# Summing four expert answers per token: four VectorE additions against one fetch and three adding transfers

## The reference, cut to what matters

```python
gath = y[sorted_e, jnp.minimum(pos, CAP - 1)]              # every answer of an expert
out = jnp.zeros((T, Hq), x.dtype).at[tok].add(gath * wv[:, None])   # four answers per token are summed
sh = jax.nn.sigmoid(x @ w_shared_gate) * (jax.nn.silu(x @ sw_gate) * (x @ sw_up) @ sw_down)
x = x + jnp.tanh(g_ffn[0]) * (... out + sh ...)
x = x + jnp.tanh(g_xattn[1]) * _L1_xattn_ref(..., _layernorm(x, axis=-1), ctx_2048)
```

## Time and profile before

| what | us |
|---|---|
| median of three runs (lowest, highest) | 1172.74 (1171.52, 1173.14) |
| the profiled execution, first to last instruction (its span) | 1171.5 |
| TensorE busy (share of the span) | 1066.6 (91%) |
| VectorE busy | 956.1 (82%) |
| ScalarE busy | 892.2 (76%) |
| GpSimd busy | 702.5 (60%) |

### The profile page before, as it was taken

The page is one execution under the profiler, slowest core; times in us unless marked ns, Lnnn a source line. Parts: engine busy times, 40 slices in busy tenths (PEclk is TensorE's granted clock), DMA queues, the critical chain, the costliest instruction groups (busy, mean ns, idle before and its releaser), DMA issues.

```text
span 1171.5 us, 24138 instructions
## 1 busy us (share of the span) xinstructions
PE 1066.6 (91%) x8396; PEld 608.8 (52%) x8396; DVE 956.1 (82%) x1748; ACT 892.2 (76%) x1546; POOL 702.5 (60%) x626
## 2 busy tenths in 40 slices
PE   8988898889988988898889988999999999999995
PEld 5743444444444444444444447756654455557774
DVE  6999999999999999999999996853328888843335
ACT  4779999999999999999999996635534567734440
POOL 3016888888787878787878785457641001543331
PEclk9999999999999999999999999799999999999998
DMA  6797987888788888888776664867937003433326
GB/s 192 121 163 146 171 171 162 171 171 173 161 171 171 173 164 173 173 169 164 155 118 110 112 109 65 244 182 213 316 98 300 1 0 85 138 102 101 102 89 222
DMA packets 388928, 176.36 MB, mean 151 GB/s; under 512 B 330542, under 2 KB 373779, under 8 KB 388809
## 3 DMA queue, kind: packets, MB, share of 16 engines
q1 hardware_dynamic: 382104, 157.85, 62.2%
q0 software_dynamic: 6480, 16.77, 4.2%
q10 hardware_dynamic: 224, 0.20, 0.1%
HBM read 52.70 MB, written 43.59 MB: 82 GB/s over the span
## 4 chain that ended last, share of the span: by engine, by line
PE 51%; DVE 33%; ACT 5%; issue 5%; DMA 3%; POOL 2%; SPq 1%; POOLq 0%; ACTq 0%; DVEq 0%
DVE top L426 26%; PE bank L234 10%; PE bank L220 9%; PE bank L1187 4%; PE bank L2599 4%; PE bank L252 4%; PE bank L1580 3%; PE bank L2615 3%; PE bank L1174 2%; PE bank L1166 2%; ACT weight L485 2%; PE bank L270 1%; PE bank L1598 1%; PE bank L682 1%; POOL dispatched_rows L1823 1%
## 5 line engine op out<-in xcount | busy, mean ns | idle before, releaser
L485 ACT ACTIVATE weight<-bank,bias,sq_all 128x1024 uint8<-128x1024 f32 x512 | 610.2, 1201 | 24.1 <-PE bank L234 18.9
L426 DVE TENSOR_REDUCE top<-bank 128x1 f32<-128x512 f32 (+1 forms) x683 | 610.1, 951 | 11.9 <-PE bank L220 1.6
L537 POOL CAST weight<-turned 128x2048 bf16<-128x2048 uint8 x256 | 479.4, 1895 | 44.8 <-PE bank L252 23.2
L234 PE MATMUL bank<-kT,query 128*128 128x512 bf16 x1024 | 307.7, 382 | 11.8 <-ACT weight L485 4.8
L252 PEld LDWEIGHTS bank<-v_sb,weight 128*128 128x128 bf16 x4096 | 172.0, 97 | 103.4 <-POOL weight L537 1.9
L220 PE MATMUL bank<-kT,qspace 64*128 64x512 bf16 x687 | 134.9, 386 | 55.0 <-DVE top L426 55.0
L252 PE MATMUL bank<-v_sb,weight 128*128 128x16 bf16 x4096 | 172.5, 170 | 0.6 <-POOL weight L537 0.6
L220 PE MATMUL bank<-kT,query 128*128 128x512 bf16 x337 | 127.8, 379 | 1.6 <-DVE top L426 1.4
L234 PEld LDWEIGHTS bank<-kT,query 128*128 128x128 bf16 x1024 | 59.8, 96 | 103.8 <-ACT weight L485 61.8
L1823 POOL DMA_INDIRECT dispatched_rows<-qspace,put x32 | 37.1, 1161 | 117.8 <-DVE qspace L2376 108.6
L485 ACT ACTIVATION_READ_ACCUMULATOR weight<-bank,bias,sq_all 128x1 f32 x512 | 101.3, 198 | 0.0
(11 more groups left out here) (350 smaller groups left out, 1466.2 us busy)
## 6 DMA issues: line engine op xcount, KB each, us to landing
dispatched_rows<-zeros SPq DMA_DIRECT2D x32, 524.0 KB, 3.2
answered_rows<-zeros SPq DMA_DIRECT2D x16, 512.0 KB, 3.2
late<-answered_rows SPq DMA_DIRECT2D x16, 512.0 KB, 6.3
erow<-dispatched_rows SPq DMA_DIRECT2D x39, 131.0 KB, 2.1
wgu<-in_L_ffn_w_gate SPq DMA_DIRECT2D x26, 176.0 KB, 3.9
wgu<-in_L_ffn_w_up SPq DMA_DIRECT2D x26, 176.0 KB, 3.9
query<-qspace SPq DMA_DIRECT2D x32, 128.0 KB, 3.1
turned<-weight SPq DMA_TRANSPOSE x256, 3.1
```

Of the source, the lines that this page charges most:

```text
L234: mm = pe.matmul(unit[u % 2][:, v * 512:(v + 1) * 512], query2[:, t % 2, h, :], kT[:, h // 2, first + v * 512:first + (v + 1) * 512], star ...
L426: ve.tensor_reduce(top[:, first:first + count], bank[:, first % 3:first % 3 + count, :], AX.X, ALU.max).then_inc(s_max, 1)
L485: ac.activation(weight8[:, n % BYTES, u * 1024:(u + 1) * 1024], unit[u], ACT.Exp, bias=bias[:, n:n + 1], scale=sq_all[:, n:n + 1], accum_o ...
L537: po.tensor_copy(weight[:, n % 3, :, :, :].rearrange("p c q two -> p (c q two)"), turned8[:, n % 3, :, :].rearrange("p c q -> p (c q)").bi ...
```

## The change

The reading order of the table `answered` changes. For each group of four tiles, SyncE fetches the first choice's answers alone (one DMA, 512 KB, rows of 1 KB) into `answer_sums`, which lies in `late[:, 0:4, :]` and holds all 16 tiles. POOL then issues, for choices 1, 2 and 3 and for the four groups in turn, a DMA with `accum_op=ALU.add` that adds the answers of that choice to the same place. Each waits for the transfer before it on the same group. VectorE makes one addition of 128x1024 numbers for each group in place of four. ScalarE's `fade` and POOL's own work wait for the last adding transfer of group 0 in place of group 0's fetches. The waits at the end of the program (`finish_half`) change their counts only, as `s_got` is now raised once for each group here.

```diff
+                    def choices_added(k):
+                        return 16 * (E0 // FLYING + k - 1)
+
+                    answer_sums = late[:, 0:4, :].rearrange("p a (b c) -> p (a b) c", c=C)
+
+                    def tiles_of(g):
+                        return slice(g * G, (g + 1) * G)
+
+                    def choice_answers(g, k):
+                        return answered[g * G * P * K0:(g + 1) * G * P * K0, :].rearrange("(t p k) c -> p t k c", p=P, k=K0)[:, :, k, :]
...
-                        def fetch_answers(t):
-                            if t >= 2 * G and t % G == 0:
-                                sp.wait_ge(sm_["groups_combined"], t // G - 1)
-                            sp.dma_start(late[:, t % 8, :], answered[t * P * K0:(t + 1) * P * K0, :].rearrange("(p k) c -> p (k c)", k=K0)).then_inc(s_got[t // G], 16)
-
-                        for t in range(2 * G):
-                            fetch_answers(t)
+                        for g in range(NG):
+                            sp.dma_start(answer_sums[:, tiles_of(g), :], choice_answers(g, 0)).then_inc(s_got[g], 16)
...
-                        for t in range(2 * G, NT):
-                            fetch_answers(t)
...
-                        po.wait_ge(s_got[0], 16 * G)
+                        for k in range(1, K0):
+                            for g in range(NG):
+                                if k == 1:
+                                    po.wait_ge(s_got[g], 16)
+                                else:
+                                    po.wait_ge(s_er[g], choices_added(k))
+                                po.dma_start(answer_sums[:, tiles_of(g), :], choice_answers(g, k), accum_op=ALU.add).then_inc(s_er[g], 16)
+                        po.wait_ge(s_er[0], choices_added(K0))
...
-                        ac.wait_ge(s_got[0], 16 * G)
+                        ac.wait_ge(s_er[0], choices_added(K0))
...
-                            ve.wait_ge(s_got[g], 16 * G)
-                            for k in range(K0):
-                                settle()
-                                m = ve.tensor_tensor(x_sb[:, g * G:(g + 1) * G, :], x_sb[:, g * G:(g + 1) * G, :],
-                                                     late[:, (g % 2) * G:(g % 2 + 1) * G, k * C:(k + 1) * C], ALU.add)
-                                if k < K0 - 1:
-                                    step(m)
-                            m.then_inc(sm_["groups_combined"], 1)
+                            ve.wait_ge(s_er[g], choices_added(K0))
+                            ve.tensor_tensor(x_sb[:, tiles_of(g), :], x_sb[:, tiles_of(g), :], answer_sums[:, tiles_of(g), :],
+                                             ALU.add).then_inc(sm_["groups_combined"], 1)
```

More of the change, by code:

```diff
@@ L1138, in weights_loaded @@
                 return 64 * n + (16 if s < 2 * NG + 3 else 0)
-            s_er = [sem(f"x0_rows_fetched_{s}") for s in range(FLYING)]
+            s_er = [sem(f"x0_rows_fetched_then_answers_added_{s}") for s in range(FLYING)]
             s_er1 = s_ew[0:RING1]
@@ L2728, in experts1_vector @@
                             ve.wait_ge(sm_["shared_answers_added"], 2 * NG * G - (1 if g == 0 else 0))
-                            ve.wait_ge(s_got[g], 32 * G)
+                            ve.wait_ge(s_got[g], 16 * (G + 1))
                             finish_half(2 * g)
```

## The result

| | us |
|---|---|
| before, median (lowest, highest) of 4 | 1172.13 (1170.89, 1173.14) |
| after, median (lowest, highest) of 4 | 1205.43 (1201.75, 1206.47) |
| ratio after / before, 95% interval | 1.0277 [1.0262, 1.0292] |
| span of the profiled execution, before and after | 1171.5 and 1204.2 |

The kernel is 2.8% slower, 33.3 us by the medians and 32.7 by the two profiled spans; 1202.4 was forecast, in a range of 1183 to 1232. The profiled execution after took 1205.93 us, 1.7 more than its span, and the kernel before shows 1.7 or 1.8 in each of the runs that have both numbers. So a run's time holds a little that its span doesn't, and that 1171.5 was both a span and the shortest run was a coincidence.

A forecast was written before the change was run, and what follows sets the result against it. TensorE was taken to bound the stage from 894 us on. Group 0's late sum moves the head by 30.2 us, less 0.5 for later additions: 1172.7 + 29.7 = 1202.4 us, range 1183 to 1232.

The forecast's parts named there:

- What bounds the stage: From 894 us on TensorE sets the time; its waits to 985 us sum to 2.0 us, and VectorE follows.
- Rival (c): VectorE bounds the stage, so nine additions give back 11.0 us in full: 4.4 us faster, 1168; chance 0.04.
- the later ones: Six additions of groups 2 and 3, 7.4 us of VectorE, hidden behind TensorE: worth 0.5 us, between nothing and 0.9.
- some 10%: VectorE's slack behind TensorE from 894 us on.
- The moment of group 0's sum: Ninth in POOL's queue, complete at 913.8 us, so the head moves by 30.2 us.
- my 10.7: First fetch to group 0's sum without adding transfers: start, plain fetches and weights (8.3 us), landing (1.1).
- Read twice: An adding transfer reads destination and source: 3.1 us each, 27.9 for nine; total 1195 to 1209, chance 0.42.
- plain price: DMA engine time of a plain 0.524 MB transfer: mean of 1.38 and 1.74 us, doubled for an adding one.
- the queue hides the round trips: Three waits in POOL's order cost nothing: a group's next transfer is issued with three others still on their way.
- rival (a): An adding transfer costs a plain one's 1.38 us: 1187; 1181.6 if three round trips of 1.0 + 3.6 bound; chance 0.27.
- The clock: TensorE's restart below full clock after 31 idle us: nothing to a few us, counted as nothing.
- the move from sum to chunk 5: Group 0's sum to chunk 5's up product: 10.3 us instead of 11.25, 1.0 us gained by six additions gone.

The follow-up runs named there:

- e4: Kernel before with one of four VectorE additions per group, three choices left out, all sixteen fetches kept: 1171.48 us against 1173.09, ratio 0.9982.
- e7: Kernel before, `fade` and POOL's fills waiting for the scatters only, VectorE's group 0 additions two and two between multiplies of chunks 3, 4, 5: 1177.64 us, ratio 1.0037.
- e9: Kernel before, `fade` and fills waiting for scatters, group 0's four additions between multiplies of chunks 3 and 4, three of group 2's moved: 1170.37 us against 1172.99.
- e10: Changed kernel with group 0's adding transfers alone and first, other fetches and weights held back, VectorE's work reordered: 1181.26 us, ratio 1.0071 to the kernel before.
- e1: Changed kernel with POOL's twelve transfers copying instead of adding, same order, size and waits: 1194.45 us, ratio 1.0177 to the kernel before.
- e5: Changed kernel with 36 unused products on TensorE, filling its idle time up to the restart: 1202.47 us, ratio 1.0250 to the kernel before.
- e8: Changed kernel with the same adding bytes in 128 rows of 4 KB instead of 512 of 1 KB: 1201.22 us, ratio 1.0244 to the kernel before.
- e3: Changed kernel with the adding transfers of groups 0 and 1 issued first, then groups 2 and 3: 1195.71 us, ratio 1.0194 to the kernel before.
- e6: Changed kernel with adding transfers in pairs, unneeded fetches and weights delayed, and work on ScalarE, POOL, VectorE and TensorE reordered: 1177.22 us, ratio 1.0042 to the kernel before.
- e2: Changed kernel with 29 unused products on TensorE in its idle time, ending 5.6 us before its next work: 1205.49 us.

## Why the prediction was right

**What bounds the stage: held.** From the up product of chunk 5 to the last dispatch the distances are the same to 0.1 us, with 7.4 us of VectorE's work gone. Rival (c) is out; e4 gives 2.1 us for all twelve additions. I had taken 0.5 for the later ones; the profiles of the changed kernel and of e4 show 0.0. The slack of VectorE was larger than the "some 10%" that I wrote: 78.5 us of 91 leave 14%. One shade was missing: at the head, before 903 us, the order of VectorE's work is part of the bound, as e7 (slower) and e9 (faster) show with the same number of additions.

**The moment of group 0's sum: right in kind, two terms off.** Forecast 38.6 us after the first fetch, measured 36.2. The adding transfer cost 2.65 us and not 3.1, nine times 0.45 or 4.0 us less; what lies around them came out 1.7 us longer than my 10.7. One part can be named, the time from the last byte to the landing. I had 1.1 us (by a slip: 4.0 less 1.4 less 1.3 is 1.3). A lone adding transfer takes 6.0 us in e10; less 1.3 for POOL and 2.65 for the bytes, that leaves some 2.0 us, by estimate. The other 0.8 us stay unassigned. Read twice was the likeliest case; e1 shows 1.53 for a copy on the same queue, so that both my factor (2 for 1.73) and my plain price (1.56 for 1.53) were close. That the queue hides the round trips held: the DMA share is 1.23 or more from 888 us to the sum. The round trip itself, 4.6 us in my rival (a), is 6.0 in e10. POOL's issue, 1.3 us each in my sum, was 1.27 to 1.30.

**The clock: the term I set to nothing.** Three products, the first two and part of the third at half speed, took 10.0 us in place of 5.9, and e5 gives 3 us of the program back. With this term the move from sum to chunk 5 is explained: 1.0 less by the additions as forecast, 4.1 more by the clock, +2.9 measured. With the clock at 1.00 throughout, in e5, the distance is 10.2 us, and I had put it together as 10.3. The 1.7 us more at the end were not forecast either. The clock dips there in the changed kernel, but the stall at the first sum doesn't decide it: e5 has the dip without the stall, e8 the stall without the dip. What does is open.

**The total.** 28.8 + 2.9 + 1.7 - 0.7 = 32.7 against a forecast of 29.7: 2.4 too much for the sum's moment, 4.1 too little for the clock at the restart and 1.7 too little for the end; the scatters' 0.7 and small remainders make up the rest. That the total came out within 3 to 4 us is in part luck, since these errors have opposite signs; the cause, a group's sum that comes ninth in a queue of transfers at about twice the plain price, is not luck. "Idle for some 31 us" was 29.7.

**What the prediction didn't ask** is which part of the loss belongs to the transfers. It named the work queued behind the wait and priced it as one stall. e3 and e6 show it: 9.7 us for the order of the transfers, 18.5 for the order of the work around them (with a sum 4.2 us sooner and the clock kept up), and about 5 that stay with all twelve transfers in place.

## What to carry to other kernels

Before moving work from an engine to DMAs, look where the engine's time stood: VectorE's 14.7 us here were worth 2.1. A chain of adding transfers has a latency of its own (6 us each alone, 2.65 in a full queue), and interleaving four chains gives the first consumer the latency of nearly all of them; order them by who is needed first, and move what does not need them ahead of the wait on every engine. A long wait of TensorE can cost more than the wait: here 30 us idle cost 3 to 4 us more at the restart, by the clock. And a late difference isn't an effect of the stall because it came after it: here two runs were enough to take them apart.

## What the runs showed of the hardware

- A transfer of POOL that adds 512 KB from DRAM into SBUF runs at 197 GB/s, a copying one at 342 (e1). Rows of 4 KB instead of 1 KB make 2.5 us of 2.65 (e8, at the end of the queue). Alone, with its issue and its landing, an adding transfer takes 5.9 to 6.1 us (e10).
- POOL's instruction for such a transfer took 1.27 us for 512 rows, 0.85 for 128 (e8), and 0.75 for a copy of 512 rows (e1), while an indirect scatter of 128 rows took 0.99.
- TensorE's granted clock fell to 0.50 some 5 us after it stopped, and in e2 within the 5.6 us between the last filling product and the next work. It came back some 9 us after the restart in the changed kernel and about 4 us after it in e8: the time to come back differs from run to run.
